# Attention pipeline of a decoder layer: first transpose group moved behind the scores, and a new opening of DVE's step

## The reference

```python
x = x + attention(layernorm(x))          # 32 query heads, 8 key/value heads of 64, RoPE, causal
x = x + cross_attention(layernorm(x))    # 64 memory rows for each batch, masked
x = x + moe(layernorm(x))                # 8 experts, top 2, gated
# attention, for each query head:
attn = jnp.einsum('bkgqd,bkld->bkgql', qh, kh) * SCALE
attn = jnp.where(causal, attn, -jnp.inf)
p = softmax(attn)
out = jnp.einsum('bkgql,bkld->bkgqd', p, vh)      # then out @ Wo.T
```

## Time and profile before

| | |
|---|---|
| median of 3 runs | 1660.87 us (1659.72 to 1661.71) |
| the profiled execution's own time | 1664.38 us |
| its span in the trace | 1662.6 us |
| PE busy in the span | 1502.7 us (90%) |
| DVE, ACT, POOL busy | 1325.5, 1113.1, 1047.5 us |

### The profile page before, as it was taken

How to read it: one execution, slowest core, us unless ns; L and a number is a source line. 1 busy time by engine, 2 the same in 40 slices (tenths; PEclk the granted TensorE clock), 3 DMA queues, 4 the chain that set the end, 5 groups by cost and what they waited for, 6 DMA issues and landing times. The chain is left out here.

```text
span 1662.6 us, 31706 instructions
## 1 busy us (share of the span) xinstructions
PE 1502.7 (90%) x8951; PEld 1324.1 (80%) x8951; DVE 1325.5 (80%) x3470; ACT 1113.1 (67%) x2593; POOL 1047.5 (63%) x1161
## 2 busy tenths in 40 slices
PE   5799999999999999999999998699679999999994
PEld 4678888888888788888888887588579999999993
DVE  7788888888888788888888887377668998899882
ACT  3687887887887787887877878332156666666661
POOL 6568878878878878878878867546513222322321
PEclk9799999999999999999999999855589999999997
DMA  4000000000000000000000000112368878887775
GB/s 172 1 14 20 2 14 20 2 14 20 1 14 21 3 14 20 1 14 20 1 14 2 1 1 1 41 64 75 101 224 223 234 226 220 226 238 216 198 181 133
DMA packets 62033, 124.98 MB, mean 75 GB/s; under 512 B 20942, under 2 KB 21070, under 8 KB 61792
## 3 DMA queue, kind: packets, MB, share of 16 engines
q1 hardware_dynamic: 51408, 102.24, 19.4%
q0 software_dynamic: 10304, 20.59, 6.6%
q10 hardware_dynamic: 144, 0.07, 0.0%
HBM read 106.08 MB, written 24.71 MB: 79 GB/s over the span
## 5 line engine op out<-in xcount | busy, mean ns | idle before, releaser
L546 POOL TENSOR_SCALAR probs<-probs,row_inv 128x512 f32<-128x512 f32 (+3 forms) x512 | 302.0, 607 | 15.0 <-DVE row_inv L441 15.0
L313 ACT ACTIVATE probs<-probs,neg_max 128x512 f32<-128x512 f32 (+3 forms) x512 | 281.7, 552 | 28.3 <-DVE neg_max L434 25.3
L434 DVE CUSTOM_DVE_ANT_0 probs<-bank,causal 128x512 f32<-128x512 f32 (+3 forms) x512 | 220.7, 485 | 54.9 <-PE bank L208 53.9
L1246 POOL DMA_INDIRECT acc<-ctx_raw,idx x46 | 74.5, 1620 | 294.9 <-ACT ctx_raw L1399 280.6
L218 PE MATMUL bank<-ident,probs 128*128 128x128 f32 x1280 | 185.0, 275 | 60.0 <-DVE pt_lo L422 56.0
L422 DVE TENSOR_TENSOR pt_lo<-bank,pt_hi 128x512 fp32r<-128x512 f32 (+1 forms) x384 | 216.4, 591 | 26.3 <-ACT pt_hi L306 26.3
L218 PEld LDWEIGHTS bank<-ident,probs 128*128 128x128 f32 x1280 | 149.6, 141 | 96.5 <-DVE pt_lo L422 59.1
L537 POOL TENSOR_TENSOR rot<-rot,sin 128x512 f32<-128x512 f32 (+1 forms) x96 | 123.5, 1287 | 156.6 <-DVE rot L453 152.1
L1327 PE MATMUL bank<-xt_hi,gu_hi 128*128 128x256 f32 x736 | 208.6, 283 | 2.0 <-DVE xt_lo L422 1.5
L1327 PE MATMUL bank<-xt_hi,gu_lo 128*128 128x256 f32 x736 | 206.8, 281 | 0.0
L1327 PE MATMUL bank<-xt_lo,gu_hi 128*128 128x256 f32 x736 | 206.7, 281 | 0.0
(11 more groups left out here) (203 smaller groups left out, 4115.9 us busy)
## 6 DMA issues: line engine op xcount, KB each, us to landing
gu_raw<-in_gate_up SPq DMA_DIRECT2D x92, 512.0 KB, 4.4
dn_raw<-in_down SPq DMA_DIRECT2D x92, 256.0 KB, 3.7
w_raw<-in_wqkv SPq DMA_DIRECT2D x8, 768.0 KB, 4.4
w_raw<-in_wo_rows SPq DMA_DIRECT2D x8, 512.0 KB, 3.5
h_rows<-ln_h SPq DMA_DIRECT2D x16, 256.0 KB, 2.0
acc<-x_res SPq DMA_DIRECT2D x4, 1024.0 KB, 4.9
x_res<-in_x SPq DMA_DIRECT2D x3, 1024.0 KB, 11.2
ctx_raw<-in_ctx SPq DMA_DIRECT2D x2, 512.0 KB, 6.3
```

Source lines behind the costliest of these rows:

```text
L313: nc.scalar.activation(row, row, ACT.Exp, bias=neg_max[:, hb, i:i + 1], scale=-1.0, accum_out=row_sum[:, hb, i:i + 1]).then_inc(s["exp_don ...
L434: nc.vector.tensor_tensor_reduce(out=probs[:, hb, P_AT[i]:P_AT[i] + (i + 1) * P], in0=S_BANK[k][:, at:at + (i + 1) * P], in1=causal[:, (QB ...
L546: nc.gpsimd.tensor_scalar(row, row, row_inv[:, hb, i:i + 1], 0.0, ALU.mult, ALU.add).then_inc(s["pnorm_done"], 1)
```

## The change

Three edits in the step, with no instruction added or taken away. PE transposes unit 0 of head n-1 directly behind the scores, ahead of the projection. ACT copies unit 0's high part directly behind unit 2's of the head before, ahead of the rotated parts and of the exponentials. DVE opens its step with the low part of unit 2, with `dve_o` and with `dve_w2`, then does the masking, and then at once the low part of unit 0.

```diff
--- before.py
+++ after.py
@@ -272,6 +272,8 @@
                     pe_ptrans(pe, dn_ - 1, (r + d - 1) % 3, 2)
                 if more:
                     pe_scores(pe, n + 1, m if h < G - 1 else m + 1, (h + 1) % G, (b + (h == G - 1)) % 2)
+                if d_here:
+                    pe_ptrans(pe, dn_, (r + d) % 3, 0)
                 if h < 3 and b == 3 and next_batch:
                     pe.wait_ge(s["w1_lo_done"], 3 * g + 4 + h)
                 if h == 0 and next_batch:
@@ -290,7 +292,6 @@
                 if dh == 3 and d_last:
                     pe_wo(pe, dm - 1, (db - 1) % 2, 2)
                 if d_here:
-                    pe_ptrans(pe, dn_, (r + d) % 3, 0)
                     pe_ptrans(pe, dn_, (r + d) % 3, 1)
                 if d_begun:
                     pe_pv(pe, dn_ - 1, dm if dh else dm - 1, (d + 1) % 2, (db if dh else db + 1) % 2)
@@ -389,6 +390,8 @@
                 d_before_last = not (isinstance(g, int) and g == 0 and db < 2)
                 if d_begun:
                     act_pt(act, dn_ - 1, (d + 1) % 2, 2)
+                if d_here:
+                    act_pt(act, dn_, d % 2, 0)
                 if h == 0 and begun and front:
                     act_rope(act, m, 2, b % 2)
                 if h in (1, 2) and next_batch:
@@ -398,7 +401,6 @@
                 if h == 0 and next_batch:
                     act_vt(act, m + 1, 3 * m + 4)
                 if d_here:
-                    act_pt(act, dn_, d % 2, 0)
                     act_pt(act, dn_, d % 2, 1)
                 if dh == 3 and d_last:
                     act_wo(act, dm - 1, 2)
@@ -506,24 +508,25 @@
                 d_begun = not (isinstance(g, int) and g == 0 and d < 1)
                 d_last = not (isinstance(g, int) and g == 0 and db < 1)
                 d_before_last = not (isinstance(g, int) and g == 0 and db < 2)
-                if more:
-                    dve_masked(dve, n + 1, (r + c + 1) % 3)
                 if d_begun:
                     dve_pt(dve, dn_ - 1, (d + 1) % 2, 2)
                 if d_begun and dh % 2 == 1 and not (isinstance(g, int) and g == 0 and d == 1):
                     dve_o(dve, HEADS // 2 * g + (d - 1) // 2 - 1, ((d - 1) // 2 - 1) % 4)
+                if dh == 1 and db == 1:
+                    dve_w2(dve, g)
+                if more:
+                    dve_masked(dve, n + 1, (r + c + 1) % 3)
+                if d_here:
+                    dve_pt(dve, dn_, d % 2, 0)
                 if h == 0 and begun and front:
                     dve_q_lo(dve, m, 2, b % 2)
                 if h == 2 and next_batch:
                     dve_q_lo(dve, m + 1, 1, (b + 1) % 2)
-                if dh == 1 and db == 1:
-                    dve_w2(dve, g)
                 if h < 3 and next_batch:
                     dve_rope_in(dve, m + 1, h, (b + 1) % 2)
                 if more:
                     dve_recip(dve, n + 1, (r + c + 1) % 3)
                 if d_here:
-                    dve_pt(dve, dn_, d % 2, 0)
                     dve_pt(dve, dn_, d % 2, 1)
                 if h == 3 and next_batch:
                     dve_v(dve, m + 1, (b + 1) % 2)
```

## The result

The changed kernel takes 1731.88 us (median of 5 runs, 1731.41 to 1733.4) against 1660.87: a ratio of 1.0428, with a 95% interval of 1.0416 to 1.044. That is 71 us slower, where 50 were forecast. The span of the profiled execution is 1731.1 us.

The account below looks back on a forecast made before the run. PE was taken as the bound, busy 584.67 of 625.10 us. Ordinary batches at +1.3 us and the special ones made +5.3 a group, +41 in all; with +9 for the lock, 1660.9 became 1711 us, range 1685 to 1735.

Parts of the forecast that it names:

- the rival of POOL's scalings: POOL's scalings come late for the earlier unit 0, half a microsecond more in each h = 3: 1727 us, chance 0.03.
- the lock: In h = 2, DVE's second q_st low part waits out POOL's x_res: 0.3 us a batch, +9 us in all.
- The V transposes in h = 3: Four small transposes of V now come behind unit 0 on PE: 0.25 us, at most 0.56.
- h = 0: ACT reaches unit 2's copy at T + 1.95, so PE starts unit 0 at T + 2.93: step +1.4 us.
- eight terms: ACT's chain from PE's unit 0 in h = 3 to unit 2's copy in h = 0, summed to 5.8 us.
- h = 2: ACT reaches unit 2's copy at T + 1.21, so PE starts unit 0 at T + 2.19: step +0.65 us.
- The special batches: Batches with weight copies, weight splits or a long o_lo: +1.56, 0 and -1.5 us a group.
- the old price: Second batch, split of the output projection weights: 2.35 us before the change, taken as unchanged.
- the lock that bites harder: Rival: q_st waits fully in each batch, o_lo costs 2.4 as before, w_lo meets x_res: 1733 us, chance 0.2.
- -1.5 a group: Fourth batch: o_lo's collision with POOL costs some 0.9 us of delay in place of 2.4.
- the largest term: Step h = 0, +1.4 us: ACT late at unit 2's copy, unit 0 1.4 us behind the scores.
- this gain: Step h = 3 shortens to 5.5 us, with unit 0 at T + 1.68: step -1.2 us.

Follow-up runs that it names:

- the short accumulation: The changed kernel with POOL's accumulation of the h = 1 output tile run on 8 of 512 columns, against the changed kernel: 1724.99 us.
- its experiment: The changed kernel with step h = 0 in the old order on all three engines, against the changed kernel: 1688.81 us.

## Why the prediction was right, and where it was not

**The sign and the places were right.** PE waits behind the scores for DVE's low part in every h = 0, 1 and 2, and in h = 3 where the collision or a special batch delays DVE; the wait for w_lo is gone; ACT idles mostly 1.2 to 1.4 us ahead of unit 0's copy. PE's list of waits has none for POOL, so the rival of POOL's scalings fell. Unit 0 was forecast at T + 2.19, 2.0, 1.68 and 2.93 for h = 2, 1, 3 and 0, and came at T + 2.18, 1.89, 2.15 and 3.12, or 1.66 in h = 3 when the collision with POOL is taken out. At T + 1.66 PE doesn't wait at all, so this, and not the T + 1.51 of the prediction, is the earliest place of unit 0. In h = 2 two small errors cancel: ACT came at T + 1.29 and not 1.21, and the turn to PE took 0.89 and not 0.98 us.

**The size: 20 us short.** A group was forecast at +5.3 and, with the lock, at +6.5 us, and measured +9.1. The missing 2.6 us, times 7.75, are the 20 us. By terms, an ordinary batch without the lock took 32.10 us (first batch of the short accumulation), 2.0 more than before and not 1.3:

- *The V transposes in h = 3* were taken at 0.25 us with 0.56 as the upper bound. From unit 0 to the next T are 4.14 us in the trace, not 3.85: they cost 0.54, the upper bound. 0.29 a batch.
- *h = 0*: ACT came at T + 2.24, not 1.95. From PE's unit 0 (476.13) to this copy are 6.38 us, where eight terms had given 5.8; 0.38 us of it is a wait for DVE's o_f ahead of o_hi (481.98), which the sum left out. Against it stand the 0.29 us by which PE's part was longer. The turn to PE took 0.88, not 0.98, and the step is 0.3 over the forecast: +1.70 us, 53 us over all, where 1.4 x 31 = 43 stood in the sum. That its experiment gave 43 is chance, as the h = 0 step did not come back to 7.77 us.
- *h = 2*: 0.1 over. Unit 0 came when forecast, and the step still grew by 0.75 where the stall explains 0.67; in h = 1 the same 0.08 is covered by a stall that came 0.1 shorter.
- *The special batches*, against an ordinary one of 32.10 in the version without the lock: the second 33.86, +1.76 (forecast +2.35, the old price); the third 33.50, +1.40 (forecast +1.55); the fourth 33.53, +1.43 (forecast +0.92, since the collision of o_lo, 3.19 us long, was thought to be partly hidden). Together 0.2 below the forecast. In the fourth the h = 0 step has a granted clock of 0.85 and takes 11.5 us; where the clock does not fall (the changed kernel from 547.96) it takes 9.91, and the h = 1 behind it 9.73 instead of 8.26, so the two together are the same to 0.1 us. The clock costs the changed kernel next to nothing.
- *The lock*: 1.2 us a group forecast (9 us over all), 1.23 measured.

Four batches of 0.29 + 0.3 + 0.1 are 2.8, less 0.2: the missing 2.6.

**The rival that has the same time isn't the cause.** 1733 us stood beside the lock that bites harder. It doesn't: q_st meets x_res in two batches of four, not in each, and the collision with x_res that the experiment takes out is worth 7 to 9.5 us. The time agrees with that rival by the sum of other terms. Its sum was wrong besides: an o_lo that costs 2.4 us as before takes away the whole -1.5 a group, which is 11.6 us and not 7, so the rival stood at 1738 us.

**The reason given for the largest term failed.** The prediction said that in the old order ACT reached T + 1.21 in h = 0 "because its exponentials needed nothing but the masking", so that their new place behind unit 0's copy made it late. With the exponentials in the old place it is T + 2.16, and in a kernel in which only DVE's order in h = 3 was changed T + 2.15, or T + 1.21 where the step ahead was long again. What makes ACT late is the end of PE's stall in h = 3, which had covered it. The size came near because the sum added up ACT's whole chain, which is about as long in either order; for the reason that was given, that is luck.

**What the prediction didn't see** is that the new opening alone already costs 60 us, through a masking that now waits for ACT too and low parts that run into POOL's operations. The 60 are not a part of the 71: the stalls lie elsewhere (at the start of h = 3 there, behind the scores here), and by estimate up to 16 of them come with falls of the clock that the changed kernel hardly has. It also didn't see that the one profitable edit was in it: unit 2's low part first in h = 3 alone, which removes the stall (the forecast called this gain real) and leaves ACT's lateness where nobody waits for it.

## What to carry to other kernels

A stall on the bounding engine may be what keeps the others in time; before removing it, add up their chain from that point to their next meeting, and look who will wait there. In this kernel an operation that waited for another engine was better placed behind those that waited for nothing, except in the step in which its input was there anyway. When an order written out once serves several kinds of step, try a change in each kind alone: of four, one gained 10 us here, one cost 4, two cost over 20. And when variants of a kernel are subtracted from one another, compare their granted clocks too: part of a difference can be the clock's answer to a wait.

## What the runs showed of the hardware

**DVE against POOL.** In these traces a DVE operation with both inputs in SBUF that met a POOL tensor_tensor ended 0.54 to 0.56 us after POOL's did, almost its own 0.69 us: q_st ended at 472.45 after x_res at 471.89, o_lo at 554.57 after w_lo at 554.02. In the second case DVE's o_lo was issued at 551.38, 0.11 us ahead of POOL's x_res, and got through only after two POOL operations back to back, with no turn between them. The o_lo of 3.06 us before waited for two as well; there POOL's x_res had begun at 519.51, 0.05 us ahead of it. POOL is held up as well: x_res took 1.73 us instead of 1.29 in the version with DVE's opening alone, behind the first q_st, which DVE had begun at 467.47.

The Trainium skill, SBUF — State Buffer, section SBUF: two separate sides, says that whichever of such a DVE operation and a GpSimd operation starts first has the shared ports for its whole instruction and the other is blocked. The 1.47 us row agrees. The 3.19 us row agrees only if POOL had really begun first, which its recorded start, 0.11 us later than DVE's, does not show.

**What early transposes cost PE beyond the wait.** The transposes themselves take no longer in two parts. From start to start, eight and what follows are 0.79 us apart (443.78 to 444.57 before), the two fours 0.41 and 0.36 (467.61 to 468.02, 470.87 to 471.23 after). But the first projection product behind unit 0 takes 0.32 us to the next start, where it took 0.23 behind the scores. That is why each of h = 0, 1 and 2 grew by 0.08 to 0.09 us beyond the delay of unit 0 from T + 1.51. And with no wait recorded, unit 0 starts at T + 1.66 at the earliest, 0.15 us later than a product did in its place. Four V transposes between the two parts cost 0.54 us, since nothing hides them any more.

**The granted clock can fall after a wait of PE, and need not.** With the same 1.44 us of idle time ahead of unit 0, one h = 3 step of the kernel with PE's part alone ran at a granted 1.00 and another at 0.81; with 1.82 and 1.85 us, two steps of the opening alone ran at 1.00 and 0.77. A fall lasts some 3 us at 0.50. What decides, no run here shows. Whether it costs time depends on the step: 0.7 us net in the opening alone, next to nothing in the changed kernel, where the slowed step gives the other engines the time that PE would have waited for them in the next one.
